# Turning attention's normalised rows by a DMA with transpose instead of on TensorE, and a new order of the DMA queue, in a cross-attention and routed-FFN kernel

## What is computed

```python
x = x + xattn(layernorm(x), ctx, mask, src_mask)   # 16 heads of 64, 64 keys per sequence
x = x + ffn(layernorm(x))                          # shared net + one of 2 experts per row, hidden 2048
# xattn: q = x Wq, k = ctx Wk, v = ctx Wv
#        softmax(where(mask, q k / 8, -max)) v Wo + bo
# ffn:   relu(x sw1 + sb1) sw2 + sb2 + relu(x w1[e] + b1[e]) w2[e] + b2[e],  e = argmax(x gate)
```

## Time and profile before

| | |
|---|---|
| time, median of 3 runs | 1971.18 us (1971.15 to 1971.91) |
| time of the profiled execution | 1971.43 us |
| its span, first to last instruction | 1969.6 us |
| what lies around the span | 1.8 us |
| mean granted TensorE clock | 0.981 of full speed |
| attention's first `t_p` | 134.91 us into the span |
| PE's last matmul of attention ends | 538.57 us |
| shared net's first matmul | 564.65 us |

### The profile page before, as it was taken

The page is one execution under the profiler, slowest core; times in us unless marked ns, Lnnn a source line. Parts: engine busy times, 40 slices in busy tenths (PEclk is TensorE's granted clock), DMA queues, the critical chain, the costliest instruction groups (busy, mean ns, idle before and its releaser), DMA issues. The chain is left out here.

```text
span 1969.6 us, 34192 instructions
## 1 busy us (share of the span) xinstructions
PE 1853.3 (94%) x11712; PEld 1174.3 (60%) x11713; DVE 816.8 (41%) x1701; ACT 831.6 (42%) x1473; POOL 472.8 (24%) x443
## 2 busy tenths in 40 slices
PE   6989999999759999999999999899999999999997
PEld 5334444444335666666666666566666666666664
DVE  5977766667524343344333333322222222222221
ACT  3654555444423333334454454333333333343333
POOL 1046666666500000000000000211122211212211
PEclk9999999999979999999999999899999999999998
DMA  9224433344562223223435466641122211121200
GB/s 316 76 67 121 131 118 122 122 128 114 168 215 76 77 75 107 76 96 96 139 117 157 136 207 215 216 107 44 44 55 54 58 43 40 43 63 43 65 23 15
DMA packets 186855, 206.00 MB, mean 105 GB/s; under 512 B 87568, under 2 KB 129040, under 8 KB 186384
## 3 DMA queue, kind: packets, MB, share of 16 engines
q1 hardware_dynamic: 178848, 179.66, 29.7%
q0 software_dynamic: 7920, 25.17, 4.1%
HBM read 129.56 MB, written 58.98 MB: 96 GB/s over the span
## 5 line engine op out<-in xcount | busy, mean ns | idle before, releaser
L1000 PE MATMUL pH<-room_a,room_w 128*128 128x256 f16 (+1 forms) x6336 | 769.0, 272 | 28.8 <-PEq L337 26.1
L1012 PE MATMUL pY<-room_w,room_a 128*128 128x512 f16 (+1 forms) x3120 | 755.6, 380 | 4.6 <-DVE room_a L1031 4.6
L1000 PEld LDWEIGHTS pH<-room_a,room_w 128*128 (+1 forms) x6336 | 613.5, 98 | 209.0 <-issue 37.8
L1031 DVE TENSOR_TENSOR room_a<-room_a 128x256 f16<-128x256 f32 (+1 forms) x528 | 233.5, 442 | 912.2 <-ACT room_a L1025 912.1
L1012 PEld LDWEIGHTS pY<-room_w,room_a 128*128 128x128 f16 x3120 | 305.4, 98 | 268.5 <-DVE room_a L1031 4.8
L1023 ACT ACTIVATE room_a<-pH,e_bsel,sc 128x256 f32<-128x256 f32 (+1 forms) x272 | 151.7, 558 | 435.0 <-PE pH L1000 385.5
L1023 ACT ACTIVATE room_a<-pH,b1s,sc 128x256 f32<-128x256 f32 x256 | 144.2, 563 | 383.7 <-PE pH L1000 383.7
L1190 POOL TENSOR_TENSOR room_a<-room_a,s_brow 128x512 f32<-128x512 f32 x32 | 42.4, 1346 | 589.1 <-DVE room_a L1039 589.1
L463 PE MATMUL pO<-room_w,room_b 128*128 (+1 forms) x768 | 172.5, 381 | 5.2 <-DVE room_b L685 5.2
L1025 ACT ACTIVATE room_a<-pH,e_bsel,sc 128x256 f16<-128x256 f32 (+1 forms) x272 | 149.6, 550 | 0.0
L1025 ACT ACTIVATE room_a<-pH,b1s,sc 128x256 f16<-128x256 f32 x256 | 142.2, 555 | 0.0
(11 more groups left out here) (185 smaller groups left out, 1403.3 us busy)
## 6 DMA issues: line engine op xcount, KB each, us to landing
s_er<-in_w SPq DMA_DIRECT2D x64, 512.0 KB, 4.9
room_w<-e_split SPq DMA_DIRECT2D x8, 2048.0 KB, 17.9
rows_room<-in_x SPq DMA_DIRECT2D x32, 256.0 KB, 3.2
room_a<-in_sw SPq DMA_DIRECT2D x32, 256.0 KB, 2.8
room_b<-in_x SPq DMA_DIRECT2D x32, 256.0 KB, 2.8
s_split<-room_a SPq DMA_DIRECT2D x64, 128.0 KB, 2.6
x_scratch<-room_b SPq DMA_DIRECT2D x32, 256.0 KB, 3.0
z_split<-room_b SPq DMA_DIRECT2D x32, 256.0 KB, 3.0
```

Source lines behind the costliest of these rows:

```text
L1000: mm = q.matmul(self.pH[j % 2][:, 0:rows], w[:, k, j * P:(j + 1) * P], zt[:, u, k, 0:rows], start=(n == 0), stop=(n == 3 * KC - 1))
L1012: mm = q.matmul(self.pY[u][r][:, :], h[:, j % self.HR, r * P:(r + 1) * P], w[:, j, :], start=(j == 0 and n == 0), stop=(j == HC - 1 and n ...
L1031: q.tensor_tensor(self.hl[:, j % self.HR, 0:rows], self.hf[:, j % self.HR, 0:rows], self.hh[:, j % self.HR, 0:rows], ALU.subtract).then_in ...
```

## The change

In words:

- `normal` writes the normalised rows twice on ACT, scaled by 2^11: as float32 `xnf` and as float16, the first half of `xs`. `lo_x` on POOL subtracts them into the second half of `xs`. So the split comes before the turn, not behind it.
- `t_x` (PE), `hi_x` (ACT) and the PSUM tile `pX` are gone. `turn_x` on SP turns all 128x1024 float16 of `xs` into `xT` by one DMA with transpose from SBUF to SBUF, and `sim` waits for it.
- `shifts` on DVE has one more small operation (`rs1`, the scale by 2^11).
- POOL does `lo_x` first in its slot, not fifth. DVE does `gate` behind `shifts` and `shifts2`, not before them.
- SP does `turn_x` of tile t + 3 first in its slot. `load_next` stands behind `store_w` in slot 31 and loads one quarter; the other three quarters follow behind `store_z` in slots 32, 33 and 34. SP's slots are written out (`unrolled`) instead of run in a loop.

The diff, cut to its core:

```diff
+                        def turn_x(e, g, u):
+                            at_least(e, S["sim"], count(g, u) - 2)
+                            e.wait_ge(S["xl"], count(g, u))
+                            e.wait_ge(f_done, NM)
+                            e.dma_start(xT[:, u % 2, :, :], xs[:, u % 2, :], transpose=True).then_inc(S["xT_in", u % 2], 16)
...
                             for u in range(N):
-                                if last_tile(g, u):
-                                    load_next()
+                                step(sp, g, u, 3, turn_x)
...
                                 step(sp, g, u, 1, store_w)
+                                if last_tile(g, u):
+                                    load_next()
                                 step(sp, g, u, -2, store_z)
+                                if isinstance(g, int) and g == SUB // N and u < 3:
+                                    load_w1_w2(u + 1)
...
-                            for q in range(QUARTERS):
-                                load_quarter(sp, wA, s1_d, s2_d, q, 1, first_in[f"w1_in{q}"])
-                                load_quarter(sp, wA, s1_d, s2_d, q, 2, first_in[f"w2_in{q}"])
-                        groups(sp, SUB // N, body, peel_last=2)
+                            load_w1_w2(0)
+                        def load_w1_w2(q):
+                            load_quarter(sp, wA, s1_d, s2_d, q, 1, first_in[f"w1_in{q}"])
+                            load_quarter(sp, wA, s1_d, s2_d, q, 2, first_in[f"w2_in{q}"])
+                        unrolled(SUB // N, body)
...
-                        def t_x(e, g, u):
-                            e.wait_ge(S["xn"], count(g, u))
-                            at_least(e, S["xTh"], count(g, u) - 1)
-                            for k in range(KC):
-                                mm = e.transpose(pX[:, k * P:(k + 1) * P], xn[:, u % 2, k * P:(k + 1) * P], ident[:, :])
-                            mm.then_inc(S["xT"], 1)
                         def sim(e, g, u):
-                            e.wait_ge(S["xTl"], count(g, u))
+                            e.wait_ge(S["xT_in", u % 2], dma_count2(g, u))
...
-                        def hi_x(e, g, u):
...
                         def normal(e, g, u):
                             e.wait_ge(S["rs"], count(g, u))
-                            at_least(e, S["xT"], count(g, u) - 2)
-                            e.activation(xn[:, u % 2, :], xb[:, u, :], ACT.Identity, bias=shift1[:, u % 2, :],
-                                         scale=rs[:, u % 2, :]).then_inc(S["xn"], 1)
+                            if not isinstance(g, int) or N * g + u >= 2:
+                                e.wait_ge(S["xT_in", u % 2], dma_count2(g, u) - 16)
+                            e.activation(xnf[:, u % 2, :], xb[:, u, :], ACT.Identity, bias=shift1[:, u % 2, :], scale=rs1[:, u % 2, :])
+                            e.activation(xs[:, u % 2, 0:DM], xb[:, u, :], ACT.Identity, bias=shift1[:, u % 2, :],
+                                         scale=rs1[:, u % 2, :]).then_inc(S["xn"], 1)
...
                         def lo_x(e, g, u):
-                            e.wait_ge(S["xTh"], count(g, u))
-                            e.tensor_tensor(xTl[:, u % 2, :, :], xTf, xTh[:, u % 2, :, :], ALU.subtract).then_inc(S["xTl"], 1)
+                            e.wait_ge(S["xn"], count(g, u))
+                            e.tensor_tensor(xs[:, u % 2, DM:2 * DM], xnf[:, u % 2, :], xs[:, u % 2, 0:DM], ALU.subtract).then_inc(S["xl"], 1)
```

More of the change, by code:

```diff
@@ L236, in sems @@
                         S[n] = a.enter_context(nc.semaphore("a_" + n))
-                sems("const_in", "src_neg", "stats", "rs", "xn", "xT", "xTh", "xTl", "sim", "drop", "neg", "smask", "mx", "sub", "exp",
+                sems("const_in", "src_neg", "stats", "rs", "xn", "xl", "sim", "drop", "neg", "smask", "mx", "sub", "exp",
                      "sum", "rcp", "least_set", "half_set", "prob", "pT", "pTh", "pTl", "att", "x1", "stats2", "rs2", "z", "gd", "pick1",
@@ L243, in xattn_ffn @@
                         S[n, u] = a.enter_context(nc.semaphore(f"a_{n}{u}"))
-                for n in ("r_in", "sw_in", "sw_out"):
+                for n in ("r_in", "sw_in", "sw_out", "xT_in"):
                     for u in range(2):
@@ L256, in xattn_ffn @@
                 swl = take([2, DM], F16)
-                xn = take([2, DM])
-                xTh = take([2, KC, P], F16)
-                xTl = take([2, KC, P], F16)
+                xnf = take([2, DM])
+                xT = take([2, 2 * KC, P], F16)
+                xs = take([2, 2 * DM], F16)
                 tg = take([4, KEYS], I32)
@@ L286, in xattn_ffn @@
                 rsz = sb("rsz", [P, 2, 1], F32, a)
+                rs1 = sb("rs1", [P, 2, 1], F32, a)
                 ve = sb("ve", [P, 2, 1], F32, a)
@@ L440, in sim @@
                                 for k in range(KC):
-                                    for xt, f in ((xTh, fmh), (xTh, fml), (xTl, fmh)):
-                                        mm = e.matmul(pS[u % 2][:, h * 512:(h + 1) * 512], xt[:, u % 2, k, :],
+                                    for c, f in ((k, fmh), (k, fml), (KC + k, fmh)):
+                                        mm = e.matmul(pS[u % 2][:, h * 512:(h + 1) * 512], xT[:, u % 2, c, :],
                                                       f[:, k, bass.ds(b, 1), h * 512:(h + 1) * 512],
@@ L471, in body @@
                                 step(pe, g, u, 2, sim)
-                                if not first_tile(g, u, 3):
-                                    step(pe, g, u, 3, t_x)
                                 step(pe, g, u, 0, attend)
@@ L668, in body @@
                             for u in range(N):
+                                if not first_tile(g, u, 3):
+                                    step(pool, g, u, 3, lo_x)
                                 step(pool, g, u, 2, negate)
@@ L711, in shifts @@
                             at_least(e, S["xn"], count(g, u) - 2)
-                            e.scalar_tensor_tensor(out=shift1[:, u % 2, :], in0=mv[:, u % 2, 0:1], scalar=-1.0, in1=rs[:, u % 2, :],
+                            e.tensor_scalar(rs1[:, u % 2, :], rs[:, u % 2, :], LN_SCALE, None, ALU.mult)
+                            e.scalar_tensor_tensor(out=shift1[:, u % 2, :], in0=mv[:, u % 2, 0:1], scalar=-LN_SCALE, in1=rs[:, u % 2, :],
                                                    op0=ALU.mult, op1=ALU.mult).then_inc(S["rs"], 1)
@@ L896, in body @@
                                 step(dve, g, u, -1, shifts2)
+                                step(dve, g, u, -1, gate)
                                 step(dve, g, u, -1, pick)
```

10 lines of the change are left out of this document (removed).

## The result

The kernel now takes 1951.36 us (median of 4, 1949.51 to 1952.47) against 1971.24 in the same sitting: a ratio of 0.9898, 95% interval 0.9880 to 0.9915, so 19.9 us faster. The forecast was 1917 with a range of 1910 to 1938. The sign was right, but of the 54 us that were forecast 20 came.

A forecast was written before the change was run, and what follows sets the result against it. PE was taken to bound the kernel, with idle time from an in-order chain ahead of `sim` and at the border. Slots' 43.7 us plus border's 10.7 us made 54.4 us, from 1971.4 to 1917 us, range 1910 to 1938.

The forecast's parts named there:

- So neither is next to bind: Attention slots: POOL's 8.5 us and DVE's 9.0 + 0.15 us of work fit in a slot of 11.3 us.
- the moved gate under "Nothing": DVE in attention: moving the gate behind the shifts costs nothing, as its result is used in the next stage.
- Theory B: Stated before the experiments, for the changed kernel's slots: DVE simply has too much work, whoever runs beside it.
- A, z's store binds: Rival for attention's slots: slow landing of z's store holds `residual`, slot 12.0 us, total 1937 us; chance 15%.
- PE's bound of 11.23 us and `t_x`'s 0.44: PE in attention: without `t_x`, 0.44 us a slot, `t_p`, `sim` and `attend` sum to 11.23 us with no wait.
- The turned tile is in time: Ahead of `sim`: the tile lands at 16.9 us, is needed at 22.5, so cover is 5.6 us.
- D: Rival for `turn_x`: a transpose's eight 128x128 blocks go one after the other, slot 12.7 us, total 1958 us; chance 4%.
- rival B: Attention: an in-order wait on POOL or SP keeps about 0.9 us ahead of `sim`, total 1948 us; chance 4%.
- E: Rival: transposes land late, waiting in the one queue; at 19.2 us the slot is 16.4, total 2065 us; chance 8%.
- The border: From attention to the shared net: z's store no longer queues behind 8 MB of weights, gain 10.7 us.
- C: Rival: the border gives nothing, as the weights' tail holds SP until the same time, total 1928 us; chance 7%.
- The start: First sims trade `t_x`, `hi_x` and their queueing for 3.2 us of landing: 0, give or take 1.5 us.

The follow-up runs named there:

- experiment 1: The changed kernel plus one wait: POOL's `sub` held back until the slot's shifts are done; 1931.98 us, ratio 0.9802.
- experiment 10: The changed kernel with the second operation of `shifts` and `shifts2` reading one tensor, the other factor a per-partition scalar; 1926.81 us, ratio 0.9782.
- experiment 6: The changed kernel with `shifts2` ahead of `shifts` on DVE, two lines exchanged; 1940.85 us, ratio 0.9850.
- experiment 2: The changed kernel with DVE's gate back ahead of `shifts` and `shifts2`; 1996.36 us, ratio 1.0125 to the kernel before.
- after: The kernel with the whole change, 1951.36 us, ratio 0.9898 to the kernel without it.
- experiment 5: The changed kernel with two edits: `sub` waits for `shifts2`, and `store_z` goes first in SP's slot; 1922.90 us, ratio 0.9759.
- experiment 11: The changed kernel with the shifts' second operations as `tensor_scalar` and `store_z` first in SP's slot; 1919.37 us, ratio 0.9743.
- experiment 9: The changed kernel with `sub` waiting for `shifts2`, `store_z` first, and `turn_x` moved seven DMAs later, behind `store_w`; 1922.33 us, ratio 0.9756.
- experiment 3: The kernel without the change, given only the border's part: `load_next` behind `store_w`, weights in four parts; 1961.84 us, ratio 0.9952.
- before: The kernel without the change, 1971.24 us in the sitting of the main result; the experiments are timed against it.
- experiment 7: The kernel without the change, with only the gate moved behind `shifts` and `shifts2`; 1954.90 us, ratio 0.9922.
- experiment 8: The kernel without the change, with the gate behind the shifts and the border's new order, TensorE's transposes kept; 1945.30 us, ratio 0.9877.
- experiment 4: The changed kernel with `store_z` of tile t - 2 first in SP's slot, ahead of `turn_x`; 1946.57 us, ratio 0.9875.
- experiment 12: The changed kernel with `lo_x` back behind `norm` in POOL's slot; 2111.26 us, ratio 1.0712.

## Why the prediction went wrong, by its own steps

- **"So neither is next to bind" (POOL and DVE), and the moved gate under "Nothing": the step that failed.** The sum took 11.3 us a slot; it measured 11.55 in slot 4 and 12.6 from there on, 31 us less gain in all. The work was counted with the durations of the earlier trace rows, where POOL stood idle as the shifts ran. The prediction itself put `sub` at 8.3 us and the shifts at 8.0 to 8.5, beside each other, and didn't ask whether they could run so. L711 went from 0.15 to 1.87 us, on the chain `shifts2`, `normal2`, `normal`, `hi_p`, `lo_p`, `attend`. It was named only as what could make the prediction wrong, without a price or a chance. Experiments 1 and 10 remove it in two ways and get 19 and 24 us back; experiment 6 moves it; experiment 2 makes two stalls of it, 1.78 and 1.13 us. Theory B is refuted: 10 does the same work and gives DVE waits again.
- **A, z's store binds:** not what set the slot of after, but right as the next loop. With the lock gone, `residual` waits for it, and the slot is 11.5 to 11.6 instead of 11.23, where I had 11.3 and an upper end of 12.0. The store landed after 4.1 us by the median, not 3.0; the upper end stood for 4.4. Experiments 5 and 11 take it away for 9 and 7 us.
- **PE's bound of 11.23 us and `t_x`'s 0.44:** right, slots 1 to 3 of after and all of experiment 11. The forecast's whole sum for the slots, 340.7 us, stands against 338.8 there.
- **The turned tile is in time:** right. It lands 3.1 us after issue by the median (3.2 from the earlier trace rows); PE waits for one once, 5.4 us at the start. Experiment 9 confirms the cover. In experiment 11 `turn_x` goes out 14.2 us after the start of `sim` (298.44 to 312.64), against 13.7 in the prediction. D is refuted, eight blocks land together. Its price was also read from a line that counts 32 plain loads: the 33 transposes of the earlier trace rows alone land after 3.1 us at least, not 2.6 (3.2 by the median as before), so a block's price was 1.8 us and D's time some 2016 us, as an estimate, not 1958. Refuted is also the rival B of the prediction (not the theory), as no wait is left ahead of `sim`. E did not happen.
- **The DMA engines' share:** 0.53 against 0.58 foretold, and 0.57 at the faster slot of experiment 11.
- **The border:** mechanism right, 8.7 us for 10.7; PE idle 15.93 us for 15. C is refuted (experiment 3 gives 9.8).
- **The start:** mis-sized. The first `t_p` came 2.2 us later, beyond the 1.5 allowed. With TensorE's transposes it came at 133.1 to 135.4 us (before and experiments 3, 7 and 8), with the turned tiles at 137.1 to 139.1, in all ten runs. Not tried by itself.
- **1919.37 us in experiment 11 lies near the forecast of 1917 in part by luck:** the slots gave 45.6 us (43.7 foretold), the border 7.3 (10.7), the later stages 2.3 (0), and the start cost 3.6 (0).

## What to carry to other kernels

A gain that comes from removing a wait moves other instructions beside each other that never were: go through the pairs on DVE and POOL that will start at one event, and look whether DVE's reads two tensors from SBUF. A tiny instruction is no exception; give it a per-partition scalar in place of the second tensor, or let the long one wait for it. A clean stretch of slots doesn't show that the two engines keep clear of each other: in experiment 4 hundredths of a us decided it. And an in-order queue with a wait at its head passes that wait on to all that stands behind (experiments 4 and 12), so the entry with most slack can go last (experiment 9).

## What the runs showed of the hardware that I had not expected

- A DVE instruction on 128x1 took 1874 ns beside a POOL instruction of 1.90 us with both reading SBUF, and 149 ns without it. The form with one tensor operand took 204 ns by the median and 206 at most, beside `norm` (299.85 in experiment 10) as where POOL stood idle when it began (149.07).
- It is symmetric: POOL's 128x1024 `sub` went from 1.90 to 2.40 us when DVE's gate of 0.74 us had started 0.11 us ahead (experiment 10).
- The slow slot holds itself once entered. The same program ran slots of 11.23 us and then of 12.6 in one execution (experiment 4), which no average over the stage shows.
